# Output matrix multiplied into the recurrent input matrices, and one variance product per encoder step

## Chip, cores and metric

The kernel runs on one core of a Trainium2 chip. The metric is the device time of one execution in microseconds (us), as the median of several runs; less is better.

## What is computed

A small vision tower: 64 images are cut into patches and projected (tokens), go through one attention layer, and then through four experts whose outputs are mixed with a router's weights. The part that matters here is one expert, with D = 256 and 16 heads of 16; tokens is 64 images x 65 positions = 4160.

```python
def _expert(x, p):
    h = _ln(relu(x @ ew1 + eb1) @ ew2 + eb2, eg, ebeta)        # encoder
    q, k, v = split(h @ aiw + aib)                              # attention, 16 heads
    o = softmax(q @ k.T * SCALE) @ v
    h = o @ aow + aob                                           # output matrix aow
    hf = _lstm_dir(h, wif, whf, bf)                             # zg = xt @ Wi + h @ Wh + b
    hb = _lstm_dir(h[:, ::-1], wibk, whbk, bbk)[:, ::-1]
    mem = concatenate([hf, hb])                                 # then gates, decoder, layer norm
```

The two recurrences (forward and backward) run over the 65 positions. Everything is float32 at the interface; several products are done as three float16 products of a high and a low part (`PASSES`).

## The kernel before, in words

The program is a row of stages, each one block in which the five engines (PE, DVE, ACT, POOL, SP) run their own instruction lists and wait for each other by semaphores; between two blocks every engine resets and raises semaphores. The order of the work is written out by hand. The stages: tokens, first attention, a norm, the experts' stage, the LSTM stage (four experts together), the head.

**The experts' stage** (`experts_stage`) loops over the four experts. For each it does:

- the *encoder*: 10 steps of 416 tokens (`WIDE`), laid out as a pipeline in `laid_steps`. In a step PE multiplies by the first matrix (L1260, 2 products), by the second, whose columns have their mean taken off (L1269, 4 products), and sums the squares over the features with a constant matrix `mean` (L1276, 2 products, one for each half `kk` of the 256 features). ACT does the relu (L1408), the root (L1414) and the squares (L1419, both halves in one instruction); DVE adds the bias (L1374) and takes the reciprocal of the root (L1382); POOL multiplies it in (L1197). Between the steps, DVE and PE prepare the expert's weights (the functions in `between`); there the output matrix is copied to `w_out` (L1322).
- the *attention* (`ImageAttention`): units of four images, 16 units, with a few steps of lag for each later operation. In step s of a unit PE projects the values (L694), scores an image (L746), transposes an earlier image's weights (L757) and weighs the values (L770); once a unit it projects the keys and queries of the next unit (L672, in steps 1 and 2) and does the class token (L776, L703, in step 3). DVE takes the maxima (L859), shifts (L864), sums (L870), inverts (L872), and once a unit splits the next unit's input into high and low float16 parts (L826, L828), which PE's L672 waits for. POOL masks the keys (L629) and multiplies by the inverse (L658). ACT does the exponential (L946) and copies out of PSUM; L916 keeps the attended values in `ax_o`.
- the *output product*: for each unit PE multiplies `ax_o` by `w_out` (`pe_out`, L708, at s == 0 and s == 3, for the unit two before), ACT stores the result with its bias in `x_out` (L1431), and DVE takes the largest magnitude of each unit (`largest`, L1388). At an expert's end SP saves `x_out` to DRAM (4.2 MB).

**The LSTM stage** (`lstm_stage`) first prepares 16 matrices of 1 MB (input and recurrent, two directions, four experts) in four buffers: DVE measures each (L1657), sizes a power-of-two scale for each pair in a chain of small instructions (L1669 to L1682, with two small PE products), ACT scales (L1764) and rounds to float16 (L1769), POOL subtracts to get the low part (L1571), and only then SP reloads the buffer (L1444). Then come 65 time steps: PE multiplies `l_xs` and `l_hs` by the weights (L1591), DVE adds the bias (L1696), and so on.

```python
for e in range(EXPERTS):                       # PE, before the time steps
    pe.wait_ge(w_low, BASE + 4 * (e + 1))
    products(0, e, True)
```

## Time and profile before

| | us |
|---|---|
| median of 3 runs | 4080.25 |
| lowest, highest | 4079.73, 4081.5 |
| the profiled execution: its own time | 4074.98 |
| its span, first to last instruction | 4073.3 |

| stage (of the profiled execution) | about, us |
|---|---|
| tokens, first attention, norm | 0 to 435 |
| experts' stage: four times encoder and attention | 435 to 1729 |
| recurrent weights prepared | 1732 to 1852 |
| the 65 time steps | 1852 to 3284 |
| head | 3284 to 4073 |

| engine | busy us | share | instructions |
|---|---|---|---|
| PE | 3618.4 | 89% | 35696 |
| PEld (weight loads) | 2221.2 | 55% | 35696 |
| DVE | 2791.8 | 69% | 4905 |
| ACT | 2178.6 | 53% | 4312 |
| POOL | 1239.3 | 30% | 1020 |

The stages are told apart by the first and last start of their lines. A float32 product shows as two records of PE, so the 256 output products of the four experts are 512 records. In a timeline row the bracket at the end is the idle time before the instruction and what ended it.

### The profile page before, as it was taken

How to read it: one execution, taken by the hardware profiler on the slowest of the kernel's cores; microseconds unless marked ns; L12 is line 12 of the kernel's file. 1: busy time of each engine (PE TensorE's matmuls, PEld its weight loads, DVE VectorE, ACT ScalarE, POOL GpSimd, SP SyncE). 2: the span in 40 equal slices, each digit the busy share in tenths (PEclk: the TensorE clock that was granted, in tenths of full speed). 3: DMA queues.
4: the chain of work that ended last, by engine and by line, in shares of the span. 5: the costliest groups of instructions: out<-in, count | busy, mean ns of one | idle time of the engine just before them, and what ended most of it. 6: DMA issues, size and time to landing. Idle time of an engine off the chain costs nothing. (4 is left out here: it accounts for less than half of the span.)

```text
span 4073.3 us, 95960 instructions
## 1 busy us (share of the span) xinstructions
PE 3618.4 (89%) x35696; PEld 2221.2 (55%) x35696; DVE 2791.8 (69%) x4905; ACT 2178.6 (53%) x4312; POOL 1239.3 (30%) x1020
## 2 busy tenths in 40 slices
PE   6877799989989889807999999999999949999997
PEld 5744456556556556504555555555555537666665
DVE  7866688688688688766666666666666664555555
ACT  6856367557657657754444444444444454555554
POOL 0035367367457447651000000000000003444443
PEclk8989899999999999958999999999999969999999
DMA  9910100100100100062111111111111131111111
GB/s 183 188 24 16 46 13 0 44 16 0 43 16 1 43 32 1 6 196 76 49 46 50 49 44 49 46 50 49 44 49 46 49 109 41 54 55 55 55 55 31
DMA packets 392915, 205.36 MB, mean 50 GB/s; under 512 B 151221, under 2 KB 386474, under 8 KB 392106
## 3 DMA queue, kind: packets, MB, share of 16 engines
q1 hardware_dynamic: 392354, 203.09, 19.5%
q8 instruction: 104, 1.70, 0.2%
q14 instruction: 65, 0.53, 0.0%
q10 hardware_dynamic: 392, 0.03, 0.0%
HBM read 145.55 MB, written 57.51 MB: 50 GB/s over the span
## 5 line engine op out<-in xcount | busy, mean ns | idle before, releaser
L1591 PE MATMUL banks<-l_w,l_xs 128*64 128x512 f16 x6240 | 721.1, 381 | 15.1 <-DVE l_xs L1639 14.2
L1591 PE MATMUL banks<-l_w,l_hs 128*64 128x512 f16 x6144 | 705.7, 379 | 1.7 <-DVE l_hs L1645 1.7
L1591 PEld LDWEIGHTS banks<-l_w,l_xs 128*64 128x64 f16 x6240 | 343.9, 110 | 330.5 <-issue 24.6
L1591 PEld LDWEIGHTS banks<-l_w,l_hs 128*64 128x64 f16 x6144 | 348.1, 110 | 316.9 <-DVE l_hs L1645 2.2
L194 POOL MEMSET h_ident<- 128x128 f32 x1 | 0.2, 205 | 1443.5 <-POOLq L81 1443.5
L1752 ACT ACTIVATE l_gates<-l_gates 128x768 f32<-128x768 f32 x260 | 219.3, 843 | 354.2 <-DVE l_gates L1696 354.2
L658 POOL TENSOR_TENSOR ax_p<-ax_p,ax_ri 128x520 f32<-128x520 f32 (+1 forms) x256 | 320.2, 1252 | 274.7 <-DVE ax_ri L872 274.7
L1696 DVE SCALAR_TENSOR_TENSOR l_gates<-banks,l_unscale,l_bias 128x1024 f32<-128x1024 f32 x260 | 333.8, 1284 | 99.4 <-PE banks L1591 97.5
L2023 PE MATMUL banks<-h_mem,h_w 128*128 128x320 f16 x2496 | 357.5, 300 | 0.0
L2318 ACT ACTIVATE h_work<-banks,h_bias,h_factor 128x320 f32<-128x320 f32 x312 | 192.4, 617 | 260.6 <-PE banks L2023 256.8
L1756 ACT ACTIVATE l_ig<-l_cell 128x256 f32<-128x256 f32 x260 | 108.3, 417 | 353.9 <-DVE l_cell L1713 351.9
L2023 PEld LDWEIGHTS banks<-h_mem,h_w 128*128 128x128 f16 x2496 | 245.0, 98 | 92.8 <-issue 0.3
L629 POOL TENSOR_TENSOR ax_km<-ax_k,ax_mask 128x512 f32<-128x512 f32 x256 | 291.1, 1137 | 5.4 <-PE banks L746 5.4
L946 ACT ACTIVATE ax_p<-ax_p 128x520 f32<-128x520 f32 (+1 forms) x256 | 170.5, 666 | 212.1 <-DVE ax_p L864 210.9
L672 PE MATMUL banks<-ax_x,w_in 128*128 128x256 f16 (+1 forms) x1632 | 200.1, 276 | 63.6 <-DVE ax_x L828 44.7
L1709 DVE TENSOR_TENSOR l_ig<-l_gates 128x256 f32<-128x256 f32 x256 | 109.0, 426 | 210.1 <-ACT l_gates L1753 210.1
L859 DVE TENSOR_REDUCE ax_mx<-banks 128x8 f32<-128x520 f32 (+1 forms) x256 | 186.0, 727 | 83.8 <-PE banks L746 83.5
L864 DVE TENSOR_TENSOR ax_p<-banks,ax_mx 128x520 f32<-128x520 f32 (+1 forms) x256 | 187.9, 734 | 34.4 <-DVE ax_mx L859 19.5
L672 PEld LDWEIGHTS banks<-ax_x,w_in 128*128 128x128 f16 x1632 | 147.9, 101 | 103.2 <-DVE ax_x L828 57.0
L317 PE MATMUL banks<-packed,w_cols 128*128 128x256 f32 x672 | 160.0, 401 | 47.4 <-ACT packed L345 47.4
L1717 DVE TENSOR_TENSOR l_hid<-l_gates,l_ig 128x256 f32<-128x256 f32 x260 | 110.8, 426 | 130.2 <-ACT l_ig L1756 130.2
L870 DVE TENSOR_REDUCE ax_sm<-ax_p 128x8 f32<-128x520 f32 (+1 forms) x256 | 183.9, 718 | 0.0
(334 smaller groups left out, 6957.7 us busy)
## 6 DMA issues: line engine op xcount, KB each, us to landing
l_x<-x_scratch SPq DMA_DIRECT2D x130, 256.0 KB, 3.0
mem_scratch<-l_hs SPq DMA_DIRECT2D x520, 64.0 KB, 1.9
h_mem<-mem_scratch SPq DMA_DIRECT2D x104, 320.0 KB, 3.7
image<-in_x_dram SPq DMA_DIRECT2D x132, 196.0 KB
x_scratch<-x_out SPq DMA_DIRECT2D x4, 4160.0 KB, 16.4
ring<-in_x_dram SPq DMA_DIRECT2D x60, 196.0 KB
raw_in<-in_L_ffn_attn_in_w_dram SPq DMA_DIRECT2D x4, 768.0 KB, 4.5
h_scratch<-x_out SPq DMA_DIRECT2D x1, 2080.0 KB, 6.5
```

The costliest lines, as they stand in the source:

```text
L629: pool.tensor_tensor(self.km[:, s % 2], self.k[:, par, :, s, :].unsqueeze(2).broadcast_to([P, KD, 4, self.KEYS]), self.mask4[:, :].unsquee ...
L658: pool.tensor_tensor(self.p[:, v, :, 0:k], self.p[:, v, :, 0:k], self.ri[:, v, :, 0:k].unsqueeze(3).broadcast_to([P, 2, k, SEQ]), ALU.mult ...
L672: mm = pe.matmul(bank, w_in[:, k, b, at:at + P], x[:, a, k], start=(k == 0 and i == 0), stop=(k == KD - 1 and i == len(PASSES) - 1))
L859: dve.tensor_reduce(self.mx[:, s % 2, :, 0:k], now, AX.X, ALU.max).then_inc(self.maxed, 1)
L864: dve.tensor_tensor(self.p[:, v, :, 0:k], now, self.mx[:, s % 2, :, 0:k].unsqueeze(3).broadcast_to([P, 2, k, SEQ]), ALU.subtract).then_inc ...
L870: dve.tensor_reduce(self.sm[:, v, :, 0:k], self.p[:, v, :, 0:k], AX.X, ALU.add).then_inc(self.summed, 1)
L946: act.activation(self.p[:, s % 4, :, 0:k], self.p[:, s % 4, :, 0:k], ACT.Exp, scale=SCALE).then_inc(self.exped, 1)
L1591: mm = pe.matmul(ps[d * HALF:(d + 1) * HALF, 2 * z + n, :], lhsT, w_of[e][:, d, kk, b, n * 512:(n + 1) * 512], start=(kk == 0 and turn_ == ...
L1696: dve.scalar_tensor_tensor(out=gz.rearrange("p (n c) -> p n c", n=2), in0=ps[:, 2 * z:2 * z + 2, :], scalar=unscale[:, e:e + 1], in1=bias[ ...
L1752: act.activation(gates[:, z, 0:3 * D], gates[:, z, 0:3 * D], ACT.Sigmoid).then_inc(gated, 1)
L2023: mm = pe.matmul(ps[:, bank, 0:W], w[:, e, b, here:here + P], moving(k, a), start=(k == 0 and turn_ == 0), stop=(k == nk - 1 and turn_ == 2))
L2318: act.activation(dst[:, m, :], ps[:, bank, 0:W], func, bias=bias(m), scale=factor[:, e, at:at + 1]).then_inc(S[name + "_kept"], 1)
```

## The change

1. **Output matrix folded in.** Since h = o @ aow + aob is only read as h @ Wi, the experts' stage no longer forms h: ACT writes the attended values (with v's class part as before) straight into `x_out` (`keep`), and the LSTM stage's x is o. `PROJECTED = False` takes `pe_out`, its stores and `largest` out of the experts' attention; the first attention stage (`PairAttention`) keeps its own. In the encoder's preparation PE now transposes the output matrix (four 128 x 128 transposes) and DVE keeps it in `early.out_t` for each expert; the bias product goes to `shared.out_bias`.
2. **New preparation of the LSTM's weights.** For each expert PE multiplies the output matrix into both input matrices in float32 (`fold`, four parts of four 128 x 512 products) and forms the bias as rows (`bias_rows`, 12 products of 64 rows). DVE measures the four matrices and the output matrix and sizes one chain per expert with a bound of the product; ACT rounds the folded parts out of PSUM (`high_part`), DVE takes the low parts from PSUM (`low_part`), and only the recurrent matrices (8, not 16) go through ACT's two instructions and POOL's subtraction. Six matrices are loaded ahead instead of three, into memory lent by the stage before, and the rest into buffers that are free earlier.
3. **Encoder.** POOL adds the two halves of the squares, and PE does one product instead of two.

The core of the diff (semaphore lists and memory layout left out):

```diff
@@ ImageAttention, PE @@
-                if s == 0 and self.unit_in(u, -2):
+                if self.PROJECTED and s == 0 and self.unit_in(u, -2):
                     pe.wait_ge(self.o_kept, BASE + (unit - 1) * GROUP)
                     pe.wait_ge(self.out_kept, BASE + (unit - 2) * KD)
                     self.pe_out(pe, ps, w_out, par, 0)
...
@@ ImageAttention, DVE @@
-                if s == 1 and self.unit_in(u, -3):
-                    dve.wait_ge(self.out_kept, BASE + (unit - 2) * KD)
-                    largest(at - 3)
@@ experts_stage, ACT @@
-                def store(at, m, bank, b):
-                    dst = xo[:, :, m, ds(at * GROUP, GROUP)].rearrange("p t b -> p b t")
-                    return act.activation(dst, bank.rearrange("p (b t) -> p b t", t=SEQ), ACT.Identity, bias=b)
+                def keep(par, b, at, c):
+                    return xo[:, :, c, ds(at, 1)].rearrange("p t b -> p (t b)")
@@ encoder, POOL @@
+                    if live(1):
+                        pool.wait_ge(squared, BASE + e * STEPS + k)
+                        pool.tensor_tensor(sq[:, 1 - par, 0], sq[:, 1 - par, 0], sq[:, 1 - par, 1], ALU.add).then_inc(halved, 1)
@@ encoder, PE @@
-                        pe.wait_ge(squared, BASE + at - 1)
+                        pe.wait_ge(halved, BASE + at - 1)
                         pe.wait_ge(rooted, BASE + at - 2)
-                        for kk in range(KD):
-                            mm = pe.matmul(ps[:, 4, 0:WIDE], mean[:, :], sq[:, par, kk, :],
-                                           start=(kk == 0), stop=(kk == KD - 1))
-                        mm.then_inc(varied, 1)
+                        pe.matmul(ps[:, 4, 0:WIDE], mean[:, :], sq[:, par, 0, :], start=True, stop=True).then_inc(varied, 1)
@@ lstm_stage, PE @@
+            def fold(e, u):
+                v, d, m = 4 * e + u, u // KD, u % KD
+                if v >= PARTS:
+                    pe.wait_ge(f_low, BASE + v - PARTS + 1)
...
+                for n in range(2):
+                    for k in range(KD):
+                        mm = pe.matmul(ps[:, part_bank(v) + n, :], out_t[:, e, k, m * P:(m + 1) * P],
+                                       stage[4 * e + d][:, k, n * 512:(n + 1) * 512], start=(k == 0), stop=(k == KD - 1))
+                mm.then_inc(folded, 1)
...
             for e in range(EXPERTS):
-                pe.wait_ge(w_low, BASE + 4 * (e + 1))
+                fold(e, 0)
+                pe.wait_ge(measured, BASE + SIZES * (e + 1))
...
+                pe.transpose(ps[0:SIZES, 7, 0:P], most[:, e, :], ident[:, :]).then_inc(most_turned, 1)
+                fold(e, 1)
+                pe.wait_ge(sizing, BASE + SIZING * e + 2)
+                pe.matmul(ps[:, 7, 2 * P:2 * P + SIZES], ones[:, :], diag[:, :], start=True, stop=True).then_inc(most_shared, 1)
+                fold(e, 2)
...
+                fold(e, 3)
+                bias_rows(e)
@@ lstm_stage, DVE @@
+            for e in range(EXPERTS):
+                if e + 1 < EXPERTS:
+                    measure_out(e + 1)
+                for u in range(4):
+                    low_part(e, u)
+                    if e + 1 < EXPERTS:
+                        measure(e + 1, u)
+                if e + 1 < EXPERTS:
+                    size(e + 1)
@@ lstm_stage, ACT @@
+                high_part(e, 0)
+                high_part(e, 1)
+                high_own(e, 0)
+                high_part(e, 2)
+                if e == 3:
+                    act.wait_ge(w_low, BASE + 7)
+                high_own(e, 1)
+                high_part(e, 3)
```

The order of instructions at three places. First PE in the attention's loop, at the end of a unit (step 3, then the head of step 0; names are memory tiles); before:

```order
L757 MATMUL banks<-x_ident,ax_p 128x128 x4
L770 MATMUL banks<-ax_pt,ax_v 32x65 x8
L776 MATMUL banks<-x_ident,ax_p 64x128 x2
L703 MATMUL banks<-ax_k,ax_qc 32x64 x16
L708 MATMUL banks<-ax_o,w_out 128x260 x2
L733 ISA
L734 REGISTER_ALU
```

and now:

```order
L758 MATMUL banks<-x_ident,ax_p 128x128 x4
L771 MATMUL banks<-ax_pt,ax_v 32x65 x8
L777 MATMUL banks<-x_ident,ax_p 64x128 x2
L710 MATMUL banks<-ax_k,ax_qc 32x64 x16
L734 ISA
L735 REGISTER_ALU
L701 MATMUL banks<-w_in,ax_x 64x128 x12
```

The output product between the class products and the next unit's values is gone, and nothing stands in its place.

Second, POOL in the encoder's steps now (before, only the rows that write `x_h` were there):

```order
L1201 TENSOR_TENSOR x_h<-ring,x_rs 128x2x416
L1197 REGISTER_ALU
L1198 TENSOR_TENSOR ring<-ring 128x416
L1201 TENSOR_TENSOR x_h<-ring,x_rs 128x2x416
L1197 REGISTER_ALU
L1198 TENSOR_TENSOR ring<-ring 128x416
```

An addition of 416 columns stands ahead of each multiplication.

Third, PE in the preparation of one expert's recurrent weights (`out_t` is the turned output matrix, `ring` and `plot` hold the loaded matrices). Before, PE had two small products there for each pair of matrices:

```order
L1612 MATMUL banks<-l_ident,ring 3x128
L1614 MATMUL banks<-ring 128x3
L1612 MATMUL banks<-l_ident,ring 3x128
L1614 MATMUL banks<-ring 128x3
L1612 MATMUL banks<-l_ident,ring 3x128
```

Now, for one expert:

```order
L1664 MATMUL banks<-plot,out_t 128x512 x4
L1687 MATMUL banks<-l_ident,ring 5x128
L1664 MATMUL banks<-plot,out_t 128x512 x4
L1690 MATMUL banks<-ring 128x5
L1664 MATMUL banks<-plot,out_t 128x512 x8
L1674 MATMUL banks<-ring,plot 64x512 x2
L1678 MATMUL banks<-plot 64x512 x4
L1674 MATMUL banks<-ring,plot 64x512 x2
L1678 MATMUL banks<-plot 64x512 x4
```

Four folds and the bias rows come round for each expert, with the two small products between them. The time steps' own instructions stand as before.

## Rows read from the trace of the kernel before

**Rows 1.** Busy time by stretch: window, length, then PE, PEld, DVE, ACT, POOL, clock
```profile
850.93:864.52 13.59, 11.93 (x223) 7.96 (x221) 12.18 (x21) 9.79 (x26) 10.42 (x9) 1.00 0.01 2
964.47:979.15 14.68, 14.00 (x231) 9.28 (x230) 12.72 (x22) 10.71 (x29) 10.47 (x10) 1.00 0.00 0
1095.20:1148.50 53.30, 51.81 (x157) 28.30 (x157) 43.70 (x44) 23.77 (x36) 15.57 (x8) 1.00 0.01 3
1731.70:1852.10 120.40, 7.65 (x24) 4.62 (x24) 78.58 (x114) 64.50 (x37) 65.39 (x19) 0.50 0.56 164
1852.10:3284.00 1431.90, 1429.17 (x12897) 745.58 (x12897) 962.56 (x2058) 591.92 (x1289) 0.00 (x0) 1.00 0.19 50
```

**Rows 2.** Timeline of PE in unit 1 of the second expert: start, length, engine, line
```profile
856.28 1.48 PE L672 MATMUL banks<-ax_x,w_in 128*128 128x256 f16 x12 [0.68 <-DVE ax_x L828]
...
861.56 0.66 PE L746 MATMUL banks<-ax_km,ax_q 64*64 64x256 f32 x8
...
864.52 0.66 PE L746 MATMUL banks<-ax_km,ax_q 64*64 64x256 f32 x8
```

**Rows 3.** The same in a later unit of the second expert, with the output product
```profile
954.48 1.14 PE L708 MATMUL banks<-ax_o,w_out 128*128 128x260 f32 x4
...
963.59 0.66 PE L746 MATMUL banks<-ax_km,ax_q 64*64 64x256 f32 x8
...
966.09 1.14 PE L708 MATMUL banks<-ax_o,w_out 128*128 128x260 f32 x4
...
967.62 0.66 PE L746 MATMUL banks<-ax_km,ax_q 64*64 64x256 f32 x8
```

**Rows 4.** Instructions of line L828 (durations ns min/median/max)
```profile
L828 DVE SCALAR_TENSOR_TENSOR ax_x<-ax_x x64: 691/1432/1435, 493.4 to 1693.4; 128x512 f16<-128x512 f32 x64
```

**Rows 5.** Timeline from the second expert's last image to the third's first step
```profile
1074.07 0.52 ACT L916 ACTIVATE ax_o<-banks,ax_v 128x65 f32<-128x65 f32 x2 [0.64 <-PE banks L770]
...
1079.79 0.70 DVE L1388 TENSOR_REDUCE peak<-x_out 128x520 f32 x1 [3.16 <-ACT x_out L1431]
...
1081.60 3.14 PE L1260 MATMUL banks<-z,raw_w 128*128 128x416 f32 x4 [2.66 <-issue]
```

**Rows 6.** Timeline at the start of the LSTM stage's block
```profile
1731.71 0.20 POOL L194 MEMSET l_ident<- 128x128 f32 x1 [13.18 <-POOLq L81]
```

**Rows 7.** Groups by line: encoder (whole span)
```profile
L1276 PE MATMUL banks<-ring,x_mean 128*128 128x416 f32 x160 | 62.8, 515 | 5.9 <-ACT ring L1419 5.9
...
L1382 DVE RECIPROCAL x_rs<-ring 128x416 f32<-128x416 f32 x40 | 110.0, 2749 | 5.8 <-ACT ring L1414 5.7
...
L1197 POOL TENSOR_TENSOR x_h<-ring,x_rs 128x832 f32<-128x832 f32 x40 | 79.1, 1977 | 242.0 <-DVE x_rs L1382 242.0
```

**Rows 8.** Timeline of PE in an encoder step of the third expert
```profile
1131.72 2.96 PE L1269 MATMUL banks<-ring,w 128*128 128x416 f32 x8
...
1135.91 1.56 PE L1260 MATMUL banks<-z,raw_w 128*128 128x416 f32 x4
```

**Rows 9.** Groups by line: the recurrent weights prepared (1731.7 to 1852.1); L1696 and L1752, whole span
```profile
L1764 ACT ACTIVATE ring<-ring 128x2048 f32<-128x2048 f32 x12 | 24.0, 2000 | 54.0 <-DVE l_unscale L1682 54.0
...
L1769 ACT CAST l_w<-ring 128x2048 f16<-128x2048 f32 x12 | 22.8, 1897 | 3.5 <-DMA x_scratch<-x_out 3.2
...
L1571 POOL TENSOR_TENSOR l_w<-ring,l_w 128x2048 f16<-128x2048 f32 x12 | 48.6, 4068 | 54.4 <-ACT l_w L1769 54.4
...
L1657 DVE TENSOR_REDUCE ring<-ring 128x1 f32<-128x2048 f32 x12 | 27.3, 2280 | 9.6 <-DMA ring<-in_L_ffn_lstm_wh_f_dram 8.2 <-DMA ring<-in_L_ffn_lstm_wi_f_dram 1.4
...
L1673 DVE TENSOR_SCALAR ring<-ring 128x3 int32<-128x3 int32 x8 | 13.3, 1660 | 0.3
...
L1696 DVE SCALAR_TENSOR_TENSOR l_gates<-banks,l_unscale,l_bias 128x1024 f32<-128x1024 f32 x260 | 333.8, 1284 | 99.4 <-PE banks L1591 97.5 <-issue 0.3
...
L1752 ACT ACTIVATE l_gates<-l_gates 128x768 f32<-128x768 f32 x260 | 219.3, 843 | 354.2 <-DVE l_gates L1696 354.2
```

More of the change, by code:

```diff
@@ L513 @@
 class ImageAttention:
+    PROJECTED = False
     COUNT = IMAGES
@@ L1681, in _ @@
[L1681 to L1683 removed]
+                then(dve.tensor_scalar(scale[:, e, 0:2], total[:, :], x_inv[:, e:e + 1], None, ALU.mult), after=False)
+                then(dve.tensor_scalar(scale[:, e, 2:4], total[:, :], 1.0 / TOP, None, ALU.mult), after=False)
+                for d in range(2):
+                    rows = slice(d * HALF, (d + 1) * HALF)
+                    then(dve.reciprocal(unscale[rows, e:e + 1], total[rows, d:d + 1]), after=(d == 1))
```

365 lines of the change are left out of this document (226 added, 139 removed).

## Prediction

> **What bounds the kernel now.** I read the busy time by stretch first, since the shares of the whole span mix four different limits. In the 65 time steps PE works 1429 of 1432 us, at full clock, and POOL not at all [rows 1]: what the change touches elsewhere can't move this stretch, and its instructions stay, so 1432 us stand as they are. In the experts' attention PE leads too, but less clearly: a unit that runs the output product takes 14.68 us, 14.00 of them PE's, while DVE has 12.72, ACT 10.71 and POOL 10.47 [rows 1]. The encoder is PE's with DVE behind it (51.81 against 43.70 in 53.30 us). The preparation of the recurrent weights is nobody's by share: 120.40 us hold 78.58 of DVE, 64.50 of ACT, 65.39 of POOL and 7.65 of PE, whose clock is 0.50 there, the lower of its two levels, 1.2 GHz [rows 1]. That is a chain through all engines. Next I read timelines at the places where these limits meet.
>
> **The attention's units.** The trace of before holds what the change makes of a unit: unit 1 of every expert has no output product, since that product lags two units. It takes 13.59 us with PE at 11.93 [rows 1]. In a later unit one product (four records, 1.14 us) stands between the last image's work and the next unit's first score: from score to score 967.62 - 963.59 = 4.03 us [rows 3], in unit 1 864.52 - 861.56 = 2.96 us [rows 2]. That difference, 1.07, is the whole difference of the units, 14.68 - 13.59 = 1.09. The other product, at 954.48 [rows 3], therefore buys nothing: near it PE waits anyway, 0.68 us ahead of L672, for DVE's second split of the input (L828) [rows 2]. That split takes 0.69 us at best and 1.43 as a rule [rows 4], with POOL at work beside it. So I count one product of the two: units 2 to 15, 14 x 1.07 x 4 experts = **60 us**. Bounds: 28 products x 1.14 x 4 = 128 if both came in, and nothing if another engine took the place of PE. The stores' removal makes ACT lighter, and its copies of the attended values now go into `x_out` with a stride between elements. I cost that at nothing: ACT has 10.71 of 14.68 us [rows 1]. The cover is some 3 us a unit; if it were gone, each unit would lose what lies above it.
>
> **The attention's end.** In the second expert the last image is kept at 1074.07 + 0.52 = 1074.59 us. Then come the output product, its store, and the largest magnitude at 1079.79, until 1080.49; PE opens the third encoder at 1081.60 after a gap of 2.66 us [rows 5]. Without these three the new expert can start after about 1074.6 plus the same gap of some 2 us: 4.9 us earlier, three times 14.7. In the fourth expert nothing but the block's end follows, which comes 1080.49 - 1074.59 = 5.9 us sooner. Together **21 us**.
>
> **The encoder.** Its window of 53.30 us holds 157 records of PE, two for a product, so 0.68 us for each, and eight in a step: 5.4 us. (The products' own group reads 515 ns a record [rows 7], but records overlap; four products in 2.96 us and two in 1.56 are the same size [rows 8].) One product in eight goes: 10 x 0.68 = 6.8 us per expert, less four transposes and some copying in the preparation, under 1 us. But DVE is next: it is busy 43.70 us of the 53.30 [rows 1], the reciprocal alone 2.75 us in each step [rows 7], and has weight preparation between. If PE's time fell by 6.8, DVE would be at 94%, with a handshake in each step. I take a step of 5.2 instead of 5.4, some 2 us per expert, **8 us** in all. POOL's new addition costs half of L1197's 1977 ns [rows 7], about 0.99 us in each step. It stands beside PE's products, and POOL has 15.57 of 53.30 us. What it costs is through DVE: a DVE instruction that meets POOL takes 1.43 instead of 0.69 us [rows 4], and small ones in the preparation average 1.66 us [rows 9]. Bounds: all of PE's gain, 25 us, and a loss of 12, where half of a 0.74 us delay in eight steps of four experts is paid.
>
> The Trainium skill, "SBUF — State Buffer", section "Who interferes with whom", speaks against this addition: DVE's second port pair is shared with GpSimd, and whichever starts first holds it for its whole instruction. By that rule each of DVE's copies between the steps could wait a full addition, 8 x 0.99 x 4 = 32 us, and the encoder would lose 24 instead of gaining 8. L828's two durations agree with the rule; how often it bites here no row of before can tell.
>
> **The recurrent weights.** Before: from the block's first work at 1731.71 [rows 6] to the first time step 120.4 us. Sixteen matrices (the rows show twelve of them; the four in another buffer read alike) each take ACT 2.00 + 1.90 us, POOL 4.07 and DVE 2.28 [rows 9]. After, eight matrices do. The new work per expert:
> - Fold: 4 parts of 4 float32 products of 512 columns, at full clock 4 x 0.68 x 512 / 416 = 3.4 us for a part, at half clock 6.7. Bias rows: 12 products of 512 columns, taken in pairs side by side, 5.2 us.
> - ACT: four parts rounded out of PSUM, each 843 x 1024 / 768 = 1.12 us by L1752, and two own matrices at 3.90: 4.5 + 7.8 = 12.3 us.
> - DVE: four low parts like L1696, 4 x 1.28, and four measurements, 4 x 2.28, the output matrix 0.6: 14.8 us and the sizing chain. POOL: 2 x 4.07 = 8.1 us.
>
> No engine has more than some 20 us per expert at full clock; but sizing expert e + 1 stands behind expert e's last low part. So a period is ACT's 12.3, the last low part 1.3, the last measurement 2.3, then the transpose behind fold 1 (3.5), the shared product 0.3 and the short instructions of the sizing 1.4: 21.1 us. The first sizing is ready after about 17.5 us (3 to open, 9.7 of measuring, 3.4 for the fold that stands between the two small products, the rest the chain of small instructions), and the last expert ends about 19 us after its sizing (12.3 of ACT, 4.07 of POOL, the rest waiting for buffers). 17.5 + 3 x 21.1 + 19 = 100 us: a gain of **20 us**. The transfers don't set this: DMA is at 0.56 now [rows 1], and as many bytes are loaded, part of them sooner. Bounds: ACT alone, 17.5 + 4 x 12.3 + 4 = 71 us, a gain of 49; and PE at half clock, below.
>
> **Sum:** 60 + 21 + 8 + 20 = 109 us off 4074.98, the profiled execution's own time: 3966. The median of the runs shown is 5.3 us above that execution, so I say **3971 us**. A measurement of this kernel tells about 0.2%, 8 us, from no change.
>
> **Rivals.**
> - *PE at half clock in the preparation.* For: that stretch is at 0.50 now, and four records of L1260 right after a pause take 3.14 us [rows 5] where they take 1.56 in the stream [rows 8]. Against: PE now gets real work there. PE would have per expert 4 x 6.7 + 10.3 + 0.5 = 38 us and be the bound: 19 more than its period of 19 at full clock, 17 more than the 21.1 of the chain, over three periods 51 us, so **4022 us**.
> - *The units shrink less.* With PE lighter, the loop from POOL's mask over DVE's maxima and splits to L672 sets the unit. Unit 1 has neither the stores nor the largest magnitude either, which is for the forecast; against it, unit 1 is the first full unit, and a steady row of such units is nowhere in the trace. Half the gain: 4001 us; none: 4031.
> - *More than forecast.* The encoder gets all of PE's gain (17 more) and the preparation runs nearer ACT's bound (half of 29): **3940 us**.
> - *Slower: the clock falls in the attention.* With 11.93 of 13.59 us at work [rows 1], PE idles 12% of every unit. If that let the clock fall to 1.2 GHz, PE would need 11.93 x 2 = 23.9 us a unit, 10.3 above 13.59 (L1260's two durations, above, are two to one). The 109 us of gain are used up after 109 / 10.3 = 11 of 64 units; all 64 give 3971 + 64 x 10.3 = **4630 us**. Against it: unit 1 idles as much, and its clock is 1.00 [rows 1].
>
> The Trainium skill, "TensorE: Matmul & The Clock Gate", section "A second HAM failure mode: psum-queue depth-cycling", tells of a kernel whose frequent short idles between groups of matmuls, with PSUM banks in rotation, made the clock go back and forth. That would be this last rival. The rows of before don't show it.
>
> **How the numbers follow.** Forecast 0.57 (3950 to 3995, by the unsettled part of the preparation and the encoder's bounds); half clock in the preparation 0.13; units shrink less 0.12; more than forecast 0.15; slower 0.03. The change's steps do happen (the order of instructions shows them), so "nothing changes" has no case of its own. The range goes from 3935, which takes in most of the case of more, to 4020, which takes in half the gain in the units and ends just short of the half clock; outside lie the slow case, most of the half clock and the extremes, under 0.2. Within 0.2% of 4080 would need 101 us of the 109 to vanish: 0.01. Slower 0.04, faster 0.95.
>
> **What would show it.** A unit of 13.6 us from the third on, with 2.96 us from score to score at its end, PE's clock 1.00 and its wait for L828 in place: then the attention's steps are right. No DVE or ACT row between the last kept image and the next encoder's first product. Encoder steps of 5.2 us, ending in waits for DVE rather than PE. The first product of the time steps about 100 us after the block's first work, with 21 us from one expert's sizing to the next; if it is 150, look at PE's clock there. The time steps 1432 us. A unit above 14 us, or the encoder's window longer than before, would prove those steps wrong; a clock of 0.50 in the attention, the whole.

## The result, and the profile after

| | before | after |
|---|---|---|
| median of 3 runs, us | 4080.25 | 3988.34 |
| lowest, highest | 4079.73, 4081.5 | 3987.37, 3988.36 |
| the profiled execution: own time, span | 4074.98, 4073.3 | 3987.37, 3985.4 |

The ratio is 0.9773, with a 95% interval of 0.9751 to 0.9796: 92 us less, where 109 had been forecast. The forecast's direction and range held. (Of the 5.3 us by which the median of before stood above its profiled execution, the changed kernel has 1.0: between the two profiled executions the gain is 87.6.) The forecast's four terms did not all come in as they were built, so the two traces are compared stage by stage first. Each boundary is an instruction that both have: the first encoder product of each expert, its first score, the identity that POOL writes at the start of the LSTM block, and the first product of the time steps.

| stretch | before | after | difference | forecast |
|---|---|---|---|---|
| start to the first encoder's first product (tokens, first attention, norm) | 435.7 | 444.6 | +8.9 | 0 |
| four encoders, first product to first score | 313.7 | 312.2 | -1.5 | -8 |
| four attentions, first score to the next encoder or block | 982.3 | 908.8 | -73.5 | -81 |
| recurrent weights prepared | 120.4 | 97.8 | -22.6 | -20 |
| from the first product of the time steps to the end | 2221.2 | 2222.0 | +0.8 | 0 |
| span | 4073.3 | 3985.4 | -87.9 | -109 |

The busy time by stretch of the changed kernel (window, length, then PE, PEld, DVE, ACT, POOL with their instructions, clock, DMA share, GB/s) answers to [rows 1]. The first two windows are two neighbouring units of the second expert's attention, then come most of the third expert's encoder, the preparation, its middle, and the time steps:

```profile
906.90:920.99 14.09, 12.06 (x224) 8.02 (x221) 12.23 (x21) 10.16 (x27) 10.59 (x10) 1.00 0.00 1
920.99:934.65 13.66, 11.98 (x224) 7.98 (x220) 12.23 (x21) 10.05 (x27) 10.59 (x10) 1.00 0.00 0
1069.07:1114.87 45.80, 44.26 (x138) 24.22 (x137) 40.13 (x42) 22.60 (x34) 23.91 (x16) 1.00 0.00 1
1665.61:1763.37 97.76, 86.93 (x238) 31.51 (x238) 67.46 (x80) 53.59 (x41) 34.72 (x15) 0.94 0.47 149
1684.00:1750.00 66.00, 65.15 (x186) 23.64 (x185) 50.10 (x58) 41.93 (x30) 24.52 (x6) 1.00 0.45 151
1763.40:3195.30 1431.90, 1429.21 (x12894) 745.28 (x12896) 962.46 (x2058) 591.99 (x1290) 0.00 (x0) 1.00 0.20 50
```

Five things are to be read in it. A unit takes 13.66 us or 14.09 in turn, not 13.59. The clock is 1.00 in these units although PE idles there, so the slow rival did not come in the changed kernel; the first unit of each attention is an exception in both kernels and is looked at below. The encoder gives PE 44.26 of 45.80 us and DVE 40.13. In the middle of the preparation PE works 65.15 of 66.00 us at full clock, where it had 7.65 of 120.40 before [rows 1]: it has become the fullest engine there, which the forecast did not have. And the time steps are what they were.

Where the units' alternation comes from shows in PE's timeline at the head of a unit. This is the start of the longer one, behind the class products:

```profile
908.82 0.65 PE L710 MATMUL banks<-ax_k,ax_qc 128*32 128x64 f32 x32
909.88 0.53 PE L701 MATMUL banks<-w_in,ax_x 128*64 128x128 f16 x12 [0.41 <-issue]
910.34 0.66 PE L747 MATMUL banks<-ax_km,ax_q 64*64 64x256 f32 x8
```

and this the same place in the shorter one:

```profile
922.90 0.65 PE L710 MATMUL banks<-ax_k,ax_qc 128*32 128x64 f32 x32
923.54 0.53 PE L701 MATMUL banks<-w_in,ax_x 128*64 128x128 f16 x12
924.00 0.66 PE L747 MATMUL banks<-ax_km,ax_q 64*64 64x256 f32 x8
```

In the longer unit PE waits 0.41 us for nothing that the profile shows. The attention's loop holds two units in its body, and the pause recurs at every second unit, five times an expert, with 0.17 to 0.42 us. In the kernel before the output product's 1.14 us of queued work stood there [rows 3], and its trace has no such pause.

The first unit, from the first score to the fifth, is not among the forecast's units (no output product runs in it), and yet it changed. The second expert's in the kernel before, then the third's and the second's in the changed kernel:

```profile
836.57:850.93 14.36, 11.91 (x148) 6.95 (x144) 10.63 (x17) 6.06 (x13) 6.73 (x6) 0.70 0.00 1
```
```profile
1134.03:1146.44 12.41, 9.86 (x149) 6.05 (x145) 10.63 (x17) 5.95 (x13) 6.73 (x6) 0.91 0.01 3
827.26:841.69 14.43, 11.98 (x149) 6.95 (x145) 10.63 (x17) 6.06 (x13) 6.72 (x6) 0.70 0.00 1
```

The products are the same. At a granted clock of 0.91 in the mean the unit takes 12.41 us, at 0.70 it takes 14.4. Before, all four experts had the slower one; now three of four have the faster one, which is 5.8 us that the forecast didn't count. The clock falls while PE waits at the encoder's end, and in these three experts it is back sooner after the attention begins.

The encoder's end in the third expert, PE's timeline. Before:

```profile
1134.52 1.56 PE L1276 MATMUL banks<-ring,x_mean 128*128 128x416 f32 x4
1140.11 1.56 PE L1276 MATMUL banks<-ring,x_mean 128*128 128x416 f32 x4
...
1147.34 1.66 PE L1276 MATMUL banks<-ring,x_mean 128*128 128x416 f32 x4 [1.49 <-ACT ring L1419]
```

and now:

```profile
1099.68 0.86 PE L1284 MATMUL banks<-ring,x_mean 128*128 128x416 f32 x2
...
1104.57 0.86 PE L1284 MATMUL banks<-ring,x_mean 128*128 128x416 f32 x2
...
1109.60 0.86 PE L1284 MATMUL banks<-ring,x_mean 128*128 128x416 f32 x2
1112.00 3.03 PE L1278 MATMUL banks<-ring,w 128*128 128x416 f32 x8 [1.54 <-DVE ring L1383]
1114.87 0.86 PE L1284 MATMUL banks<-ring,x_mean 128*128 128x416 f32 x2
1120.43 1.75 PE L1284 MATMUL banks<-ring,x_mean 128*128 128x416 f32 x2 [4.70 <-POOL ring L1198]
```

and DVE and POOL between 1110 and 1120 us:

```profile
1110.75 1.10 DVE L1383 TENSOR_SCALAR ring<-banks,b2c 128x416 f32<-128x416 f32 x2
1110.90 1.96 POOL L1201 TENSOR_TENSOR x_h<-ring,x_rs 128x832 f32<-128x832 f32 x1 [1.82 <-DVE x_rs L1391]
1111.78 1.37 DVE L827 TENSOR_SCALAR ax_x<-ax_x 128x512 f16<-128x512 f32 x1
1112.86 1.21 POOL L1198 TENSOR_TENSOR ring<-ring 128x416 f32<-128x416 f32 x1
1113.18 1.44 DVE L829 SCALAR_TENSOR_TENSOR ax_x<-ax_x 128x512 f16<-128x512 f32 x1
1114.54 2.74 DVE L1391 RECIPROCAL x_rs<-ring 128x416 f32<-128x416 f32 x1
...
1117.36 1.95 POOL L1201 TENSOR_TENSOR x_h<-ring,x_rs 128x832 f32<-128x832 f32 x1 [3.29 <-DVE x_rs L1391]
1119.32 1.06 POOL L1198 TENSOR_TENSOR ring<-ring 128x416 f32<-128x416 f32 x1
```

PE's steps did fall, from 5.59 us (1140.11 less 1134.52) to 4.89 (1104.57 less 1099.68): all of the product's 0.70, where 5.2 had been forecast. But DVE could not follow: with its instructions beside POOL's (L829 takes 1.44 us beside L1198; the same instruction of the encoder takes 0.69 in the kernel before and in both runs below that have no addition in this step) a step of DVE is 5.3 to 5.7 us, and 6.5 in the step of L829. It falls behind, and PE waits for it at the end, 1.54 us and then 4.70 for the addition, which stands behind POOL's multiplication. The last two steps, which took 4.19 and 3.04 us before, take 5.3 and 5.6.

The preparation of the second expert's weights, PE's timeline from one transpose of the sizing to the next:

```profile
1697.94 0.27 PE L1687 MATMUL banks<-l_ident,ring 128*5 128x128 f32 x1
...
1705.77 3.70 PE L1664 MATMUL banks<-plot,out_t 128*128 128x512 f32 x8 [0.17 <-DVE l_w L1777]
...
1718.68 0.27 PE L1687 MATMUL banks<-l_ident,ring 128*5 128x128 f32 x1
```

These 0.17 us are the only pause of PE in 20.74 us.

### The profile page after: what moved, and what is told of

The parts are those of the page before. It is cut to its first block and busy times, and to the rows that moved or that the text cites. A ratio compares the mean times of both kernels' runs of the same rounds, so it can differ in the third digit from the quotient of the medians.

```text
span 3985.4 us, 94491 instructions
## 1 busy us (share of the span) xinstructions
PE 3549.4 (89%) x35332; PEld 2154.8 (54%) x35332; DVE 2747.6 (69%) x4811; ACT 2115.4 (53%) x4188; POOL 1256.6 (32%) x1056
## 5 line engine op out<-in xcount | busy, mean ns | idle before, releaser
L1636 PE MATMUL banks<-l_w,l_xs 128*64 128x512 f16 x3120 | 361.9, 382 | 7.5 <-DVE l_xs L1723 6.6
L1636 PE MATMUL banks<-plot,l_xs 128*64 128x512 f16 x3120 | 359.9, 380 | 0.0
L1636 PE MATMUL banks<-l_w,out_t 128*64 128x512 f16 x3072 | 352.9, 379 | 1.7 <-DVE out_t L1729 1.7
L1636 PE MATMUL banks<-plot,out_t 128*64 128x512 f16 x3072 | 352.8, 379 | 0.0
L1870 ACT ACTIVATE l_ig<-l_kept 128x256 f32<-128x256 f32 x260 | 108.2, 416 | 357.2 <-DVE l_kept L1827 355.3
L1636 PEld LDWEIGHTS banks<-l_w,l_xs 128*64 128x64 f16 x3120 | 172.5, 110 | 166.8 <-issue 21.4
L1636 PEld LDWEIGHTS banks<-l_w,out_t 128*64 128x64 f16 x3072 | 174.0, 110 | 159.5 <-DVE out_t L1729 2.2
L1636 PEld LDWEIGHTS banks<-plot,out_t 128*64 128x64 f16 x3072 | 174.1, 110 | 157.4
L1636 PEld LDWEIGHTS banks<-plot,l_xs 128*64 128x64 f16 x3120 | 171.4, 110 | 157.7 <-issue 10.8
L324 PE MATMUL banks<-packed,plot 128*128 128x256 f32 x672 | 164.3, 408 | 54.4 <-ACT packed L352 54.4
## 6 DMA issues: line engine op xcount, KB each, us to landing
out_t<-x_scratch SPq DMA_DIRECT2D x130, 256.0 KB, 3.0
```

Source lines behind the costliest of these rows:

```text
L324: m = pe.matmul(ps[:, n % 2, 0:XI * NP], w_cols[:, q, :], packed[:, n % 2, q, :], start=(q == 0), stop=(q == WHOLE - 1))
L1636: mm = pe.matmul(ps[d * HALF:(d + 1) * HALF, 2 * z + n, :], lhsT, w_of[e][:, d, kk, b, n * 512:(n + 1) * 512], start=(kk == 0 and turn_ == ...
```

## The experiments

Each kernel was timed beside runs of the kernel before on the same chip; these read 4078 to 4081 us in the median, with single runs some 7 us to either side. Differences between kernels are therefore also given from the stretches of their profiled executions, which are sharper.

**The 8.9 us ahead of the experts.** They stand in the tokens stage, which ends at 253.3 us before and 264.3 after, and in which the DMA engines are always busy (share 1.00 between 20 and 200 us). The diff has nothing there but memory. One tile, `w_cols`, moved into borrowed memory, and the image buffers begin at 109696 bytes in each partition before, a multiple of 128, and at 121536 after, 64 over one. A line of an image is 896 bytes. The first edit, and its mirror in the kernel before, which is the same line:

```diff
+        sb("pad", [P, 16])
         own = sb("image", [ROWS, SLOTS - 1, XI, GRID, SIDE])
```

> The changed kernel itself, as the measure for the others on this chip. Its tokens stage took 264.3 us to the next stage's first instruction where the kernel before took 253.3, and the diff has no edit in it but the place of one tile. Theory 1, the image buffers' address decides the speed of their loads: the same 264 us here and about 3988 us. Theory 2, the 11 us belong to the one chip or the one execution: then 253 to 264 here, and before's own tokens stage varies too.

> The changed kernel with 64 bytes a partition left free ahead of the image buffers in the tokens stage, so that they begin at a multiple of 128 bytes again (121600; 109696 in the kernel before, 121536 in the changed one). Theory 1, the address: the loads return from 176 to 187 GB/s, the tokens stage to 253 us, the kernel to 3988 - 11 = 3977 us. Theory 2, the stage is slower for another reason (the chip, the other tile moved into the borrowed memory): 3988 us, unchanged.

> The kernel before with 64 bytes left free ahead of the same buffers, which puts them at 109760, 64 over a multiple of 128. Theory 1, the address: tokens stage 264 us, kernel 4080 + 11 = 4091 us. Theory 2: 4080 us, tokens stage 253.

> The changed kernel with the 64 bytes ahead of all borrowed memory, so that every later tile that was 64 over a multiple of 128 bytes moves too, the LSTM's and the head's with it. Theory 1 in the tokens stage alone: 3977 us, as with the image buffers alone. If other transfers gain as well (the time steps' and the head's), less than that by the gain of each; those stages took 0.9 us longer than before's in all, so at most a few us. Theory 2: 3988.

In `all_up64` the pad stands ahead of `plot` instead. In the other two it moves the tiles behind the image buffers as well. Measured, with the end of the tokens stage and the rate of its loads:

| kernel | median (runs), us | ratio to before, 95% | tokens stage ends | GB/s, 20 to 200 us |
|---|---|---|---|---|
| before (first chip run) | 4080.25 | | 253.3 | 187 |
| after_again | 3988.14 (4) | 0.9775, 0.9759 to 0.9791 | 266.5 | 176 |
| image_up64 | 3980.76 (4) | 0.9757, 0.9741 to 0.9773 | 259.9 | 181 |
| before_up64 | 4085.99 (10) | 1.0014, 1.0005 to 1.0024 | 264.2 | 178 |
| all_up64 | 3977.59 (4) | 0.9748, 0.9732 to 0.9764 | 257.7 | 182 |

The windows that the last column is from, the kernel before, then `before_up64`, then the changed kernel in `after_again`, then `image_up64`:

```profile
20.00:200.00 180.00, 139.49 (x589) 117.63 (x590) 148.92 (x49) 151.41 (x75) 6.63 (x9) 0.91 1.00 187
```
```profile
20.00:200.00 180.00, 138.29 (x554) 114.93 (x555) 141.17 (x47) 143.62 (x70) 6.40 (x9) 0.87 1.00 178
```
```profile
20.00:200.00 180.00, 133.88 (x546) 111.83 (x546) 139.60 (x47) 143.29 (x70) 5.87 (x8) 0.88 1.00 176
```
```profile
20.00:200.00 180.00, 139.22 (x558) 116.08 (x559) 142.81 (x48) 145.75 (x74) 6.61 (x9) 0.86 1.00 181
```

Every engine has the same instructions in `before_up64` as in the kernel before, and its loads are slower by 5%. The placement costs time in both kernels: 10.9 us of the tokens stage in the one, 6.6 gained back in the other (from `after_again`). Single executions scatter: in the nine profiles of kernels with the changed kernel's placement this stage, whose code is the same in all, ends between 262.2 and 271.7 us, and in the three with 64 bytes more, `combined` among them, between 256.0 and 259.9. The two groups don't overlap. The medians move less in the kernel before (5.5 us) and about as much in the changed one (7.4). `all_up64` is 3.2 us below `image_up64` in the median, of which its profile shows 2.2 in the tokens stage; that is within what single runs differ by, so nothing is claimed of the other tiles. What stays open is the rest: 257.7 to 259.9 is not 253.3. The moved `w_cols` was not tried by itself, nor was a pad that moves the image buffers alone.

The Trainium skill, "DMA: Bandwidth & Descriptors", section "How a descriptor splits into AXI transactions", offers a reason, though it tells it of what a transfer reads: a transaction moves up to 256 bytes and has to begin at a multiple of 256, so that an unaligned start costs beats of 32 bytes that carry nothing. By that rule, and as an estimate from it, lines of 896 bytes that start 0 and 128 bytes past such a multiple in turn take 28 and 32 beats, and those that start 64 and 192 past it 30 and 34. That is 32 against 30 in the mean, for two of the three buffers (the third is in another place and did not move), 4.4% in all. The rows show 5%, 187 to 178 GB/s. Here only the address that is written to moved, and the page doesn't say that the rule holds for it, so this size agrees, but no run here shows that it is the cause. The forecast had not looked at addresses.

**The attention's two products.** The forecast rests on one of the two being free. Both were put back in the changed kernel, each alone, on PE only and with an unused result; the first condition below is `spare_step0`, the second `spare_step3`:

```diff
+    def pe_spare(self, pe, ps):
+        for k in range(KD):
+            pe.matmul(ps[:, 7, 0:256], self.spare[0], self.spare[1][:, k, :], start=(k == 0), stop=(k == KD - 1))
...
+                att.spare = (mean[:, :], early.out_t[:, 0])
...
+                if not self.PROJECTED and s == 0 and self.unit_in(u, -2):
+                    self.pe_spare(pe, ps)
...
+                if not self.PROJECTED and s == 3 and self.unit_in(u, -2):
+                    if self.unit_in(u, 1):
+                        pe.wait_ge(self.q_kept, BASE + unit + 2)
+                    self.pe_spare(pe, ps)
```

> The changed kernel with a product of the output product's size (2 x 128x256 float32, result not used) put back on PE in step 0 of the experts' units, where the first of the two stood. Forecast's theory: it is covered by the wait for DVE's split, so it costs nothing: 3988, within 4. Rival, PE alone sets the unit: 14 x 4 x 1.1 = 62 us more, 4050.

> The same product put back in step 3, where the second stood. Forecast's theory: 1.07 us a unit, 14 x 4 x 1.07 = 60 us, less what the pause of 0.41 us costs that PE now shows at the start of every second unit (5 x 4 x 0.41 = 8, which the product would cover): 3988 + 52 = 4040. Rival, the unit is now set by the loop over POOL and DVE: under 30 us more.

Measured: `spare_step0` 3989.16 us (4 runs, ratio 0.9771, 0.9748 to 0.9794), against 3988 without. Its runs lie between 3975.9 and 3996.1, so the stretches are the better witness: its four attentions take 226.8, 228.7, 226.6 and 227.5 us, the changed kernel's 226.5, 228.6, 226.0 and 227.6. `spare_step3` 4050.70 us (4 runs, 0.9925, 0.9909 to 0.9942), 62 us more, where 52 had been expected. PE in a unit of `spare_step0`:

```profile
942.58 1.13 PE L727 MATMUL banks<-out_t,x_mean 128*128 128x256 f32 x4
944.10 0.66 PE L751 MATMUL banks<-ax_km,ax_q 64*64 64x256 f32 x8
946.40 1.48 PE L679 MATMUL banks<-ax_x,w_in 128*128 128x256 f16 x12 [0.69 <-DVE ax_x L835]
```

The product is there, 1.13 us long, and the wait for DVE's split is still 0.69 us behind it: it stands in a longer gap, as the kernel before had it [rows 2, 3]. In `spare_step3` the unit is 14.67 us again (scores at 936.65, 940.67, 942.73, 947.90 and so 3.42 on), 1.08 above the 13.59 of the forecast's unit. So the same 1.1 us of PE work costs nothing at one place of the unit and its whole length at the other. A product at that place also covers the pause at the loop's end, which this trace doesn't have.

The 62 us themselves are no measure of that price. From the first to the last score the four attentions take 72 us more than in the changed kernel, and the four encoders 10.9 less (301.3 against 312.2). Two neighbouring units of the second expert show where the attentions' surplus comes from, and PE's timeline in the unit ahead of them has the same:

```profile
936.65:951.32 14.67, 13.05 (x229) 8.66 (x225) 12.25 (x21) 10.12 (x26) 10.60 (x10) 1.00 0.00 0
951.32:967.56 16.24, 14.61 (x229) 9.44 (x225) 12.23 (x21) 10.73 (x27) 10.58 (x10) 0.89 0.00 0
```
```profile
929.81 2.58 PE L679 MATMUL banks<-ax_x,w_in 128*128 128x256 f16 x12 [0.93 <-DVE ax_x L837]
```

In 15 of the 52 full units with the product the clock falls to its lower level for a part of the unit, behind two pauses of PE of some 0.7 and 0.93 us, and products that take 1.48 us take up to 2.58. Such a unit is 1.6 us longer, some 23 us in all. The kernel before has units of the same length, and PE's clock is 1.00 in them. So the mechanism of the slow rival does exist in this attention. The same pauses stand in units where it does not fall; why it comes in some and not in others is open. The encoders gain from the clock as well: the second and the fourth begin at full clock here and have their first variance product after 13.5 us, against 17.1 and 17.2 in the changed kernel.

**The pause at the loop's end.** The experts' attention was written out; every instruction and its place stay as they were:

```diff
         n, base = self.UNITS, e * self.UNITS
+        if n == 16:
+            for u in range(n + 3):
+                unit(base + u, u, u % 2, u)
+            return
```

> The changed kernel with the experts' attention written out for its 16 units instead of a loop over pairs of them (the instructions and their order are the same). Theory: the units of the changed kernel alternate between 13.68 and 14.09 us because PE stands still for 0.41 us behind the loop's end, which the output product covered before; written out, five pauses of 0.41 us per expert go, 5 x 4 x 0.41 = 8 us, 3980, with every unit at 13.6 to 13.7. Rival: the pause is where code is fetched, and more code costs as much or more in fetching: 3988 or above.

Measured: 3980.53 us (4 runs, 0.9758, 0.9741 to 0.9774), 8 us less. The four attentions take 225.3, 225.4, 225.4 and 224.5 us, 900.5 in all, 8.3 less than the changed kernel's 908.8. This sum has three parts: the units from the second on are 10.6 us shorter, the second expert's first unit is one of the fast ones (2.0), and from the last score to the next encoder or block the four experts take 4.3 us more. There PE's pause without a shown reason, ahead of the third encoder, is 4.62 us instead of 3.95. A unit of it, the window of 919.33 to 932.93 us:

```profile
919.33:932.93 13.60, 11.93 (x225) 7.96 (x221) 12.10 (x21) 10.04 (x27) 10.41 (x9) 1.00 0.01 2
```

That is unit 1 of the kernel before to a hundredth [rows 1], and all units from the second on are so. The forecast's unit was right for the code without its loop. What went missing was not another engine's time but PE's own at the loop's end, which the removed product had covered. That the pause belongs to the loop is shown; what PE does in it is not. The rival, that more code costs as much again, falls by the time, though the longer pause ahead of the encoder may be a price of it.

**The encoder.**

```diff
-                    if live(1):
-                        pool.wait_ge(squared, BASE + e * STEPS + k)
-                        pool.tensor_tensor(sq[:, 1 - par, 0], sq[:, 1 - par, 0], sq[:, 1 - par, 1], ALU.add).then_inc(halved, 1)
```

is `two_products` (with PE's two products back), and `mixed7` has the addition for the first seven steps and two products for the last three:

```diff
-                    if live(1):
+                    if live(1) and k - 1 < 7:
...
+                        added = k - 2 < 7
+                        pe.wait_ge(halved if added else squared, BASE + (e * 7 + k - 1 if added else at - 1))
...
+                        for kk in range(1 if added else KD):
```

> The changed kernel with the encoder's part undone: POOL adds nothing, PE does two variance products in a step. Theory 1 (the trace of the changed kernel): PE's steps fall from 5.58 to 4.89 us with the addition, but DVE, slowed beside POOL's additions, ends late, and most of it is given back in the last two steps; the encoders took 1.1 us less each than before's while having four transposes more. Undone: about 1 to 2 us more per encoder, 4 to 8 us, 3992 to 3996. Theory 2, the forecast's (2 us per expert): +8, 3996. Theory 3, the addition costs more than it brings: faster than 3988, by 4 us or more.

> The changed kernel with POOL's addition in the encoder's first seven steps and two products in the last three, where the chain behind the last step is open. Theory 1: the last product no longer waits for the addition behind POOL's multiplication (4.70 us of waiting, of which 1.06 the addition itself), and DVE's copies at steps 7 to 9 run at their lone price (0.4 to 0.7 us less each); PE's cost is 3 x 0.70. 0 to 2 us less per expert: 3980 to 3988. Theory 2, DVE's backlog comes from the first seven steps: no gain, 3988 or up to 8 more.

Measured: `two_products` 3993.33 us (4 runs, 0.979, 0.9774 to 0.9807), `mixed7` 3983.95 us (4 runs, 0.977, 0.9753 to 0.9786). From first product to first score the second to fourth encoders take 79.1 us with two products everywhere, 77.9 with the addition everywhere, and 76.3 with the mixture. In the encoder the addition is worth 1.2 us an expert, and leaving it out of the last three steps another 1.6. The 5 us between `two_products` and the changed kernel are thus not the encoder's alone: all four first units of its attentions take 14.0 to 14.2 us at the lower mean clock, 4.7 more than the changed kernel's four. PE's timeline at the end of `mixed7`'s third encoder:

```profile
1109.77 3.03 PE L1278 MATMUL banks<-ring,w 128*128 128x416 f32 x8 [0.84 <-DVE ring L1387]
1112.64 1.56 PE L1286 MATMUL banks<-ring,x_mean 128*128 128x416 f32 x4
1116.32 2.46 PE L1286 MATMUL banks<-ring,x_mean 128*128 128x416 f32 x4 [2.12 <-ACT ring L1428]
```

PE's waits there are 0.84 and 2.12 us instead of 1.54 and 4.70, at the price of three products. The theory of a price at the end stands, and the third (the addition costs more than it brings) falls. L829 takes 0.69 us again in both kernels, where the changed kernel has 1.44. The Trainium skill, "SBUF — State Buffer", section "Who interferes with whom", had spoken against the addition: by its rule, as the prediction estimated, the encoder could have lost 24 us. The rows agree with the rule (L829's 1.44 us beside POOL's addition, 0.69 without it) but not with that sum: each of the three encoders gained 1.2 us.

**The preparation.** The forecast let each expert's sizing stand behind the second fold. That fold was moved:

```diff
-                fold(e, 1)
                 pe.wait_ge(sizing, BASE + SIZING * e + 2)
                 pe.matmul(ps[:, 7, 2 * P:2 * P + SIZES], ones[:, :], diag[:, :], start=True, stop=True).then_inc(most_shared, 1)
+                fold(e, 1)
```

> The changed kernel with PE's small product that shares the sizes moved ahead of the second fold of each expert. Forecast's theory: the next expert's sizing stands behind that fold (5.3 us for the first, at half clock, 3.6 for the others), so the preparation shortens by 4.5 at the start and by 2 to 2.5 per later expert (ACT then waits about 1 us for the fold itself): 97.8 to about 87 us, 3988 - 11 = 3977. Rival, ACT or POOL ends the period instead: at most the 4.5 us of the first expert, 3984 or more.

Measured: 3988.55 us (4 runs, 0.9774, 0.9758 to 0.9791): no gain, and the preparation takes 97.1 us instead of 97.8. The first expert's sharing product starts 10.8 us after the block's first work instead of 15.2 as expected, and the 4.4 us are lost again by the end; the distances between the sharing products are 22.7, 21.0 and 21.0 us, not 18 to 19. Since PE works 65.15 of 66.00 us of the changed kernel's middle, the next kernel also took PE work away. It leaves out 8 of the 12 bias products of each expert, so its result lacks that part of the bias:

```diff
-                                  start=True, stop=False)
-                    for k in range(KD):
-                        for d in range(2):
-                            mm = pe.matmul(ps[d * HALF:(d + 1) * HALF, 6 + n, :], spread[e // 2][:, e % 2 * KD + k, :],
-                                           stage[4 * e + d][:, k, at], start=False, stop=(k == KD - 1))
+                                  start=True, stop=True)
```

> The changed kernel with the sharing product ahead of the second fold and without 8 of the 12 bias products of each expert (the part of the bias that comes through the input matrices is left out). Theory 1, from the trace of the changed kernel, where PE works 65.15 of 66.00 us between the first and the last expert: PE is the bound there as much as the chain, and moving the product alone could bring nothing. PE's period falls by 3.9 to 16.9 us and the chain's by 2.7 to about 18: the preparation takes 97.8 - 4.5 (first expert) - 3 x 2.7 = 85 us. Theory 2, another engine (ACT, POOL, or the transfers) ends the period: 95 us or more, as with the move alone (97.1).

Measured: 3988.32 us (4 runs, 0.9778, 0.9764 to 0.9793), preparation 98.6 us. The expected 85 did not come. The second theory's number did (95 or more), but not by the engines that it names. The kernel's three periods, by stretch:

```profile
1677.70:1742.20 64.50, 56.52 (x129) 22.80 (x129) 49.22 (x57) 38.21 (x27) 24.45 (x6) 0.89 0.53 178
```

PE has fewer products (129 records; 186 in the changed kernel's middle) and is still busy for 56.52 of 64.50 us, at a granted clock of 0.89 in the mean, between its two levels of 1.2 and 2.4 GHz, instead of 1.00. PE in one period:

```profile
1697.79 0.27 PE L1683 MATMUL banks<-l_ident,ring 128*5 128x128 f32 x1 [2.02 <-DVE ring L1733]
1698.69 0.59 PE L1685 MATMUL banks<-ring 5*128 5x5 f32 x2 [0.62 <-DVE ring L1753]
1699.21 13.59 PE L1664 MATMUL banks<-plot,out_t 128*128 128x512 f32 x24
```

and ACT beside it:

```profile
1700.59 1.11 ACT L1876 ACTIVATE l_w<-banks,ring 128x1024 f16<-128x1024 f32 x1 [5.46 <-DVE ring L1762]
1705.97 1.11 ACT L1876 ACTIVATE l_w<-banks,ring 128x1024 f16<-128x1024 f32 x1 [4.26 <-PE banks L1664]
```

Without the bias products PE waits 2.02 us for DVE's last measurement, and the folds behind that pause run slower: 24 records take 13.59 us. In `share_first`, where PE has its bias products and waits 0.63 us there, the second expert's take 10.57:

```profile
1709.33 10.57 PE L1664 MATMUL banks<-plot,out_t 128*128 128x512 f32 x24
```

The second fold is now what ACT waits for, 4.26 us. So a part of the time taken off PE comes back as PE's lower clock at the very place that the move had made critical. That is the forecast's half clock, in a part of the folds. It is not all: the four experts' groups take 12.2, 13.6, 12.3 and 12.3 us, together 8 above full clock, and 13.6 us are missing from the expected 85. The rest stays open, as does whether the chain over DVE would run in 18 us at full clock. In `share_first` itself PE's work holds the period: of 21.0 us between two sharing products it stands still for 0.62.

**All that helped, together:** the 64 bytes ahead of `plot`, seven additions in the encoder, and the attention written out.

> The changed kernel with what the runs showed to help: 64 bytes ahead of the borrowed memory (-7 to -11 us), POOL's addition in the encoder's first seven steps alone (1.6 us an expert, 6), the attention's 16 units written out (8). If they add: 3988 - 9 - 6 - 8 = 3965 us. If they overlap (each shifts the phase of the others), 3970 to 3975.

Measured: 3965.42 us (5 runs, 3959.57 to 3986.87; ratio 0.9734, 0.9711 to 0.9758), 23 us under the changed kernel and 113 under these runs' own median of the kernel before (4078.34). The first product of the time steps starts at 1736.2 us instead of 1763.4. The expected sum was 3965: the gains add, as far as five runs that lie 27 us apart can tell. (In the profile the 27.2 us are 7.8 ahead of the experts, 10.7 in the encoders and 8.4 in the attentions; the encoders' share is above the expected 6, and two of them begin at a higher clock.)

## Why the prediction was right, and where not

- **What bounds the kernel.** Right for the time steps (1429.21 of 1431.90 us are PE's, as before), and for the attention, whose unit could be read off unit 1.
- **The attention's units, 60 us.** The steady unit of 13.59 us and the one free product are confirmed by `unrolled` and the two spare products. The step that was mis-sized is "the whole difference of the units": the trace's unit 1 lies outside the loop, and inside it PE pauses at every second unit, and from the second unit on the attentions take 10.6 us more than in `unrolled`. From the stretches, 54 us came, 73.5 less the 19.3 of the ends, but only 48 of them are the forecast's. The other 6 are the first units' clock, which it didn't have, and that is luck. With the loop written out the units from the second on gain 59. The forecast's own sign, "a unit above 14 us", did appear, in four units of each expert.
- **The attention's end, 21 us.** 19.3, taken from the last score to the next first product or block: 4.8, 4.4, 5.1 and 5.0 us. The working took "the same gap of some 2 us" where its row has 2.66; the sum was near all the same.
- **The copies with a stride**, costed at nothing: ACT is at 10.05 to 10.16 us of a unit, still under the others. Right.
- **The encoder, 8 us.** 1.5 came between the two traces, transposes and all: the first encoder is 1.8 longer, since less of its head runs at full clock, and the other three are 3.3 shorter together. Against `two_products` the addition brings 1.2 an expert in the encoder, where 2 had been forecast. The step that failed is the step of 5.2 us, even throughout. PE ran its steps at 4.89, DVE fell behind, and the wait came at the end, where the addition itself also stands in the chain. The lower bound, a loss of 12, was not reached.
- **The preparation, 20 us.** 22.6 came. The period was forecast as 21.1 us and is 20.8 from sizing to sizing, the first sizing was ready after 16.9 us instead of 17.5, and the last expert took 18.6 instead of 19. But the sum was right with half of the mechanism: a fold is 3.6 to 3.7 us and the bias 5.8, and in the period from 1697.94 to 1718.68 us PE stands still for 0.17, so PE is as full as the chain is long. The forecast had PE at 19. That both are near 21 is a coincidence.
- **Not in the forecast:** 8.9 us ahead of the experts. The diff was read for its instructions and not for its addresses. The spans differ by 88 us where 109 had been forecast. The 21 missing are these 8.9, 7.5 in the attentions, 6.5 in the encoders and 0.8 at the end, less 2.6 gained in the preparation.
- **The rivals.** Half clock in the preparation held for the first two folds alone (6.47 and 5.30 us; 3.70 afterwards), since PE had work all the time; `share_first_short` shows a part of what it would have been otherwise. "The units shrink less" was true in direction (48 for 60, not the half that it named) but by a pause of PE, not by POOL and DVE. The slow rival did not come in the changed kernel: outside the first units the clock is 1.00, with PE at 12.06 of 14.09 us. Its mechanism is real all the same, as `spare_step3` shows in 15 units, and "unit 1 idles as much, and its clock is 1.00" was thinner ground than it looked.

## What to carry to other kernels

Work that is removed from the bounding engine is worth only what its place is worth: the same 1.1 us were free in one step of a loop and paid in full in another. A queue of work can hide a pause at a loop's end that shows once it is gone. A steady unit should be read from inside the loop that will run it. When a change moves memory, compare the addresses of every buffer that a DMA-bound stage loads into, and when an engine's load is lightened, look for the pause that this opens and for the clock behind it. And before a kernel's extra time is divided by a count to give a price, the stretches should be compared: the 62 us of `spare_step3` looked like 56 products of 1.1 us and were 72 less 11.

## What the runs showed of the hardware

- Loads of 896-byte lines into image buffers ran at 187 GB/s with the buffers at a multiple of 128 bytes and at 178 with them, and the tiles behind them, 64 bytes further on, in otherwise equal kernels (`before`, `before_up64`).
- At the end of the attention's loop PE stood still for 0.17 to 0.42 us with no wait that the profile shows, and not at all where the loop was written out (`unrolled`) or where 1.1 us of products stood ahead of it (the kernel before, `spare_step3`).
- In `share_first` 24 records of the folds took 10.57 us behind a pause of 0.63 us. In `share_first_short`, behind pauses of 2.02 and 0.62 us, they took 12.3 to 13.6.
- In `spare_step3` PE's granted clock fell within 15 of 52 units of the attention, behind pauses of some 0.7 and 0.93 us that the other units have too, in a kernel where a unit at full clock had PE busy for 13.05 of 14.67 us. In the changed kernel, with 12.06 of 14.09, it did not fall outside the first units.
- The same first unit of an attention took 12.41 us at a mean granted clock of 0.91 and 14.43 at 0.70.
- A DVE instruction of 128x512 elements (L829) took 1.44 us beside an addition on POOL, and 0.69 without it (`two_products`, `mixed7`).
